# A graph layer and a mixture-of-experts layer on one core: the sum of squares by four transposes and a DVE sum, five second-choice scatters in two steps, pads, waits and the stage change rearranged

## The chip, the cores and the metric

The kernel runs on one core of one Trainium2 chip. The metric is the device time of one execution in microseconds (us), here as the median of several runs. The profile is of one execution; its span runs from the first to the last instruction.

## What is computed

`x` is 128 graphs of 64 nodes with 128 features (8192 tokens), `adj` a 64x64 matrix for each graph. Everything is float32.

```python
# first layer, on the layernorm of x
agg = epsilon * xn + adj @ xn
h = silu(rmsnorm(agg @ W1 + b1) * rms_weight)        # 512 wide
x = x + h @ W2 + b2
# second layer, on the layernorm of the new x: 8 experts, top 2
logits = xf @ Wg + bg
top_w, top_i = top_k(logits, 2);  top_w = softmax(top_w)
out = sum over e of w_dense[:, e] * (gelu(xf @ W1[e] + b1[e]) @ W2[e] + b2[e])   # exact gelu
x = x + out
```

## The kernel before

Each engine has its own instruction list, written by hand and joined by semaphores; no scheduler moves anything. There are two stages.

**Stage one** works on G = 16 groups of 512 tokens, one step `s` for each, in a software pipeline. TensorE (PE) aggregates group `s+3` (`aggregate`, L566), multiplies group `s+2` with the quadratic form of W1 (`quadratic`, L574), sums the products over the 128 features (`sum_squares`, L582), runs the first matmul of group `s+1` (`first_layer`, L600) and the residual and second matmul of group `s` (L607, L614). The mean square of the rmsnorm comes from that quadratic form: DVE multiplies `agg` with it (`product`, L851), `sum_squares` sums `prod` over the partitions, DVE adds epsilon (`mean_square`, L855), and GpSimd raises it to the power -1/2 (`pow_step(s)`, L435), together with the variances of both layernorms: 12 numbers per partition for s = 1 to 11, 8 for s = 12 to 14, 4 at s = 15. `spread` (L592) turns the result into a row for all partitions, by four transposes into bank 6 (QR_BANK), and `scale_agg` (L861) applies it before `first_layer` may start. `sum_squares` writes into bank 7 (SM_BANK), which it shares with `prefix` (L623 to L628), so it waits until DVE has read the last prefix (`prefix_used`).

DVE also takes the new `x` (`take_x2`, L867), normalizes, picks the two experts of each token, and turns counts from `prefix(s-1)` into row numbers (`rank_rows`, L921, and `place_rows`). In DVE's list, a loop step begins with `take_x2(s-1)`, its statistics and `mean_square(s+1)`, and ends with `rank_rows(s-1)`, which needs the `prefix(s-1)` that PE issues at the end of step `s`.

GpSimd scatters the rows of each token to two tables in device memory, by indirect DMA (`dispatch`, L446): four per group for the first choice, four for the second. First choices go out two steps later, and beside them three second choices per step from step 3 on (42 of 64 by the end). ScalarE (ACT) does silu, tanh and copies.

**Stage two** runs tiles of 128 table rows through the expert of the tile: 71 tiles of first choices, then 71 of second choices. The sync queue (SP) loads tile `i` into one of RING = 16 slots (`load_slots`, L358) once the output of tile `i-16` has been written (`added`). DVE normalizes the rows four tiles ahead (`norm_slots(i+4)`, L1052), copies the expert's W1 (`copy_block(i+3)`, L1046) and forms the output (`finish(i)`, L1121 and L1128 or L1131). PE turns the tile (`turn`, L686), then does layer 1 (L693) and layer 2 (L708). GpSimd writes the output by indirect DMA: a plain store for first choices (L458), an accumulating one for second choices (L461). Between the stores it issues the four first choices of the last group (before tiles 11 to 14) and the 22 second choices that are left: two in five tiles. Before tile 71 it waits for all 71 stores, since accumulation comes on top of them.

Unused rows at the end of each of the 16 regions (8 experts, two choices) are overwritten with `pad_rows` by SP (`pad`, L351). These 16 pads stand behind the loads of tiles 24 to 39, one behind each; the load of tile 40 waits until all have landed.

At the start ("prologue") the blocks of `adj` for groups 0 to 3 are placed by GpSimd (`place_adj`, L273), those of later groups by DVE.

The rhythm of SP in stage two before:

```python
for i in range(RING, EARLY):            # 16 to 39
    load_slots(i)
    if i >= EARLY - KE:                 # 24
        pad(i - (EARLY - KE))
sp.wait_ge(padded, 16 * (KE + TOP_K))
```

## Time and profile before

| | |
|---|---|
| median of 3 runs | 490.04 us (488.69 to 491.08) |
| profiled execution | 489.22 us |
| its span | 487.3 us |
| PE busy | 468.2 us, 96% of the span |
| DVE busy | 352.8 us, 72% |
| GpSimd (POOL) busy | 357.5 us, 73% |
| ACT busy | 263.5 us, 54% |
| granted TensorE clock, mean | 0.993 |

The profiled time is the span and 1.9 us around it. Busy shares are means over the two stages, which have different limits; a matmul in float32 shows as two records. "issue" is idle time for which the profile names no releaser.

### The profile page before, as it was taken

To read this page: it belongs to the slowest core of one execution; us is meant where nothing else is said; L and a number is where in the kernel's file an instruction comes from. 1 tells how busy PE (TensorE), PEld (TensorE's weight loads), DVE (VectorE), ACT (ScalarE), POOL (GpSimd) and SP (SyncE) were. 2 spreads that over 40 slices of the span, in tenths; PEclk is the share of its full clock that TensorE was granted. 3 is DMA by queue.
4 is the path that set the end of the run, shared out by engine and by line. 5 is a ranking of instruction groups with operands and counts; after the bars stand their busy time and mean duration, and the time that the engine had idled before them with its cause. 6 is when DMAs were issued, how large, how long until landed. Compare 5 with 4: busy or idle time off the path is not lost. (4 is left out here: it accounts for less than half of the span.)

```text
span 487.3 us, 14189 instructions
## 1 busy us (share of the span) xinstructions
PE 468.2 (96%) x3715; PEld 423.1 (87%) x3715; DVE 352.8 (72%) x1476; ACT 263.5 (54%) x829; POOL 357.5 (73%) x318
## 2 busy tenths in 40 slices
PE   8999999999999999799999899999999999999990
PEld 5687888877888877799999799999999999999990
DVE  6788888887887675698866576766767676776751
ACT  2333333333333324477777577777777777777770
POOL 4622577787877777777777777777588888888884
PEclk9999999999999999999999999999999999999997
DMA  5995122222222212332343343333254555555430
GB/s 178 363 316 178 57 72 79 73 77 62 67 68 65 78 45 65 84 80 85 97 113 107 97 112 86 86 89 91 44 69 68 73 72 73 72 69 71 55 33 6
DMA packets 54436, 44.78 MB, mean 92 GB/s; under 512 B 9506, under 2 KB 46024, under 8 KB 54360
## 3 DMA queue, kind: packets, MB, share of 16 engines
q1 hardware_dynamic: 36480, 26.11, 20.3%
q0 software_dynamic: 16592, 17.13, 17.5%
q8 instruction: 35, 0.57, 0.5%
q10 hardware_dynamic: 1288, 0.62, 0.5%
q14 instruction: 41, 0.34, 0.3%
HBM read 25.49 MB, written 19.25 MB: 92 GB/s over the span
## 5 line engine op out<-in xcount | busy, mean ns | idle before, releaser
L797 ACT ACTIVATE gelu_t<-ps,block_w 128x128 f32<-128x128 f32 x568 | 162.0, 368 | 35.9 <-PE ps L693 35.4
L446 POOL DMA_INDIRECT dispatched_rows<-payload,row_idx x128 | 124.9, 976 | 37.4 <-issue 35.9
L693 PE MATMUL ps<-slot_t,block_w 128*128 128x128 f32 x1136 | 150.7, 275 | 0.9 <-ACT gelu_t L797 0.4
L708 PE MATMUL ps<-experts,gelu_t 128*128 x1136 | 150.4, 275 | 0.4 <-ACT gelu_t L797 0.4
L693 PEld LDWEIGHTS ps<-slot_t,block_w 128*128 128x128 f32 x1136 | 138.1, 192 | 1.9 <-issue 0.8
L708 PEld LDWEIGHTS ps<-experts,gelu_t 128*128 128x128 f32 x1136 | 138.2, 192 | 0.8 <-issue 0.8
L461 POOL DMA_INDIRECT out_y<-y_out,slot_rows x71 | 112.6, 1585 | 24.6 <-issue 24.6
L458 POOL DMA_INDIRECT out_y<-y_out,slot_rows x71 | 72.0, 1015 | 23.7 <-issue 18.8
L1121 DVE TENSOR_TENSOR y_bias<-ps,block_w 128x128 f32<-128x128 f32 x142 | 41.4, 291 | 65.3 <-PE ps L708 63.5
L1046 DVE COPY block_w<-experts 128x644 f32 x142 | 73.0, 514 | 1.3 <-issue 1.3
L614 PE MATMUL ps<-w2e,hidden 128*128 128x136 f32 x512 | 69.6, 279 | 0.0
L1052 DVE TENSOR_SCALAR slot_n<-slot_rows 128x128 f32<-128x128 f32 x142 | 58.6, 414 | 8.1 <-DMA slot_rows<-dispatched_rows 7.9
L614 PEld LDWEIGHTS ps<-w2e,hidden 128*128 128x128 f32 x512 | 63.9, 190 | 0.0
L757 ACT ACTIVATE hidden<-ps,vec_cols 128x512 f32<-128x512 f32 x64 | 44.0, 687 | 32.8 <-PE ps L600 32.7
L791 ACT COPY slot_t<-ps 128x128 f32<-128x128 f32 x142 | 37.6, 265 | 40.7 <-PE ps L686 40.2
L600 PE MATMUL ps<-agg_r,w1b 128*128 128x512 f32 x128 | 59.1, 603 | 0.0
L435 POOL TENSOR_TENSOR powers<-powers_in,neg_half 128x12 f32<-128x12 f32 (+2 forms) x17 | 33.8, 1985 | 23.3 <-DVE powers_in L855 22.1
L600 PEld LDWEIGHTS ps<-agg_r,w1b 128*128 128x128 f32 x128 | 23.0, 190 | 22.6 <-issue 22.5
L686 PE MATMUL ps<-ident,slot_n 128*128 128x128 f32 x142 | 38.9, 275 | 3.3 <-DVE slot_n L1052 3.3
L770 ACT ACTIVATE agg<-ps,ones 128x512 f32<-128x512 f32 x16 | 11.0, 687 | 52.4 <-PE ps L566 52.4
L1131 DVE TENSOR_SCALAR y_out<-y_bias,slot_rows 128x128 f32<-128x128 f32 x71 | 31.1, 438 | 2.5
L607 PEld LDWEIGHTS ps<-ident_wg,xs_t 128*128 128x128 f32 x128 | 20.5, 190 | 13.9 <-issue 13.9
(146 smaller groups left out, 416.7 us busy)
## 6 DMA issues: line engine op xcount, KB each, us to landing
slot_rows<-dispatched_rows SPq DMA_DIRECT2D x142, 66.5 KB
xs<-in_x SPq DMA_DIRECT2D x16, 256.0 KB, 5.9
xs_t<-in_x_t SPq DMA_DIRECT2D x16, 256.0 KB, 3.1
experts<-in_f_w SPq DMA_DIRECT2D x16, 256.0 KB, 5.2
out_y<-y_out,slot_rows POOLq DMA_INDIRECT x142, 3.2
adj_in<-in_adj_t SPq DMA_DIRECT2D x16, 128.0 KB, 4.3
dispatched_rows<-payload,row_idx POOLq DMA_INDIRECT x128, 2.5
dispatched_rows<-pad_rows SPq DMA_DIRECT2D x18, 66.5 KB
```

The lines of the kernel that those rows point to most:

```text
L446: pool.indirect_dma_start(rows[k], bass.IndirectOffsetOnAxis(row_idx[:, g, j * TOP_K + k:j * TOP_K + k + 1], 0), payload[:, g * JT + j, 0: ...
L458: pool.indirect_dma_start(out, token, y_out[:, r, :], None, bounds_check=T - 1, oob_is_err=False).then_inc(added[r], 16)
L461: pool.indirect_dma_start(out, token, y_out[:, r, :], None, bounds_check=T - 1, oob_is_err=False, compute_op=ALU.add).then_inc(added[r], 16)
L600: pe.matmul(bank(n % H_BANKS, 0, GROUP), w1b[:, c * P:(c + 1) * P], agg_r[:, s % 2, :], start=True, stop=True).then_inc(h_done, 1)
L614: mm = pe.matmul(x2_part(j), hidden[:, c, j * P:(j + 1) * P], w2e[:, c, :], start=False, stop=(c == C - 1))
L693: mm = pe.matmul(bank((2 * i + c // 2) % FH_BANKS, c % 2 * SLOTS, SLOTS), block_w[:, i % BLOCKS, c * P:(c + 1) * P], slot_t[:, i % 2, :], ...
L708: mm = pe.matmul(bank(Y_BANK + i % 2, 0, P), gelu_t[:, i % 2, c, :], experts[:, bass.ds(at + (OW2 + c * P), P)], start=(c == 0), stop=(c = ...
L757: act.activation(hidden[:, c, :], ps[:, (C * s + c) % H_BANKS, :], ACT.Silu, scale=vec_cols[:, GRW + c:GRW + c + 1]).then_inc(hidden_ready, 1)
L797: act.activation(gelu_t[:, i % 2, c, :], ps[:, (2 * i + c // 2) % FH_BANKS, c % 2 * SLOTS:(c % 2 + 1) * SLOTS], ACT.Gelu, bias=block_w[:, ...
L1046: dve.tensor_copy(block_w[:, i % BLOCKS, :], experts[:, bass.ds(at, OW2)]).then_inc(block_ready, 1)
L1052: dve.tensor_scalar(slot_n[:, i % (AHEAD + 1), :], row[:, X2:WID], row[:, MEAN:MEAN + 1], row[:, RSTD:RSTD + 1], ALU.subtract, ALU.mult).t ...
L1121: dve.tensor_tensor(y_bias[:, i % 2, :], ps[:, Y_BANK + i % 2, 0:P], block_w[:, i % BLOCKS, OB2:OB2 + P], ALU.add).then_inc(y_chain, 1)
```

## The change

- `sum_squares` no longer multiplies with a column of ones. It transposes the four 128x128 pieces of `prod` into bank 6, and DVE sums each over its 128 features (a `tensor_reduce` of 128x512 from PSUM to 128x4) before it adds epsilon. Its wait for `prefix_used` goes; `prefix` takes it instead. `sum_squares(1)` moves behind the first half of `first_layer(0)`, since bank 6 is in use until then.
- DVE places `adj` of groups 0 to 3 as well, each while GpSimd computes the power of that group; statistics of group 3 move behind the norm of group 2.
- GpSimd issues five second choices in two steps (3 and 2 in turn) in stage one, 35 in all; 29 are left for stage two, three in five tiles.
- The wait for all stores is split: before each of tiles 63 to 69 GpSimd waits for two earlier stores (before tile 69: those of 67 and 68), and before tile 71 for those of 69 and 70.
- SP writes the 8 pads of the first choices behind every second load from 24 on, and the other 8 behind every third load from 42 on.
- At the stage change: ACT loads the table for gelu after its tanh in step 15; DVE copies the expert block of tile 0 in step 14 and normalizes tiles 0 and 1 ahead of the gate of step 15, tiles 2 and 3 and two more blocks behind it.
- ACT loads `b1_row` ahead of `w1g`.

```diff
@@ -178,12 +179,17 @@
         H_BANKS, X2_BANK, AGG_BANK, QR_BANK, SM_BANK = 3, 3, 5, 6, 7
-        MS, PR, TO = 0, 64, 192
+        PR, TO = 64, 192
         LAST_GATE, LAST_RANKS, LAST_FIRSTS = 9, 9, 11
         SECONDS_FROM = 3
-        SECONDS_LEFT = 3 * (G + 1 - SECONDS_FROM)
+        def second_of(s):
+            return (5 * (s - SECONDS_FROM) + 1) // 2
+        SECONDS_LEFT = second_of(G + 1)
         TURN_BANK, Y_BANK, FH_BANKS = 5, X2_BANK, 3
...
@@ -260,21 +265,6 @@
             return 0 <= g < G
-        def wait_adj(engine, g):
-            if g < PLACED:
-                engine.wait_ge(adj_placed, g + 1)
-            else:
-                engine.wait_ge(adj_ready, g - PLACED + 1)
-        def half_of_adj(engine, g, h):
-            half = slice(h * NODES, (h + 1) * NODES)
-            return engine.tensor_tensor(
-                adj_blocks[half, g % 4, :, half], adj_in[half, g % ADJ_RING, :, :],
-                eps_ident[half, half].rearrange("p (a n) -> p a n", a=1).to_broadcast([NODES, JT, NODES]),
-                ALU.add)
         def after(engine, semaphore, value):
...
@@ -372,15 +362,19 @@
                 load_slots(i)
-                if i == EARLY - KE:
+                if i == EARLY - 2 * E:
                     sp.wait_ge(ends_ready, 1)
-                if i >= EARLY - KE:
-                    pad(i - (EARLY - KE))
+                if i >= EARLY - 2 * E and i % 2 == 0:
+                    pad((i - (EARLY - 2 * E)) // 2)
             sp.wait_ge(tables_ready, 1)
-            sp.wait_ge(padded, 16 * (KE + TOP_K))
+            sp.wait_ge(padded, 16 * (E + TOP_K))
             sp.wait_ge(late_dispatched, 16 * JT * (G - EARLY_GROUPS))
...
                 load_slots(i)
+                if i % 3 == 0 and (i - EARLY) // 3 < E:
+                    pad(E + (i - EARLY) // 3)
+            sp.wait_ge(padded, 16 * (KE + TOP_K))
             sp.wait_ge(second_dispatched, 16 * JT * G)
...
@@ -411,14 +405,6 @@
                                    ALU.pow).then_inc(rstd1_ready, 1)
-            def place_adj(g):
-                pool.wait_ge(adj_loaded[g], 16)
-                half_of_adj(pool, g, 0).then_inc(adj_half, 1)
-                pool.wait_ge(adj_half, g + 1)
-                half_of_adj(pool, g, 1).then_inc(adj_placed, 1)
-                pool.wait_ge(adj_placed, g + 1)
             def pow_rms0():
...
@@ -461,12 +447,10 @@
                                             oob_is_err=False, compute_op=ALU.add).then_inc(added[r], 16)
+            def wait_written(i):
+                pool.wait_ge(added[i % RING], 16 * (i // RING + 1))
             pow_ln1(0)
-            pool.wait_ge(adj_clear, 1)
-            pool.wait_ge(eps_ready, 1)
-            pool.wait_ge(rstd1_ready, 1)
-            place_adj(0)
-            place_adj(1)
             pow_ln1(1)
...
@@ -474,14 +458,8 @@
             pow_rms0()
-            pool.wait_ge(pool_consts, 5)
-            pool.wait_ge(rrms_ready, 1)
-            place_adj(2)
             pow_step(0)
             pow_ln1(2)
-            pool.wait_ge(powers_ready, 1)
-            pool.wait_ge(rstd1_ready, 3)
-            place_adj(3)
             pow_ln1(3)
...
@@ -491,27 +469,32 @@
                 if s >= SECONDS_FROM:
-                    second(3 * (s - SECONDS_FROM))
+                    second(second_of(s))
                 if s == G:
...
                 if s >= SECONDS_FROM:
-                    second(3 * (s - SECONDS_FROM) + 1)
-                    second(3 * (s - SECONDS_FROM) + 2)
+                    second(second_of(s) + 1)
+                    if second_of(s) + 2 < second_of(s + 1):
+                        second(second_of(s) + 2)
             for i in range(NT):
...
                     dispatch(G - 1, i - LAST_FIRSTS, 0)
-                n = SECONDS_LEFT + (i - 1) // 5 * 2 + (i % 5 == 3)
-                if i % 5 in (1, 3) and n < G * JT:
+                n = SECONDS_LEFT + i // 5 * 3 + i % 5 // 2
+                if i % 5 in (0, 2, 4) and n < G * JT:
                     second(n)
+                if TILES - 8 <= i < TILES - 1:
+                    wait_written(2 * i - TILES)
+                    wait_written(2 * i - TILES + 1)
                 if i == TILES:
-                    for q in range(RING):
-                        pool.wait_ge(added[q], 16 * len(range(q, TILES, RING)))
+                    wait_written(TILES - 2)
+                    wait_written(TILES - 1)
                 write_tile(i)
...
@@ -560,7 +543,7 @@
                 pe.wait_ge(xn_ready, g + 1)
-                wait_adj(pe, g)
+                pe.wait_ge(adj_ready, g + 1)
                 after(pe, agg_copied, g)
...
@@ -575,12 +558,12 @@
                 pe.wait_ge(prod_ready, g + 1)
-                after(pe, ms_ready, g)
-                after(pe, prefix_used, g - 2)
+                if g == 1:
+                    pe.wait_ge(agg_r_ready, 1)
                 for j in range(JT):
-                    mm = pe.matmul(bank(SM_BANK, MS + j, 1), prod[:, j * P:(j + 1) * P], ones[:, 0:1],
-                                   start=True, stop=True)
+                    mm = pe.transpose(bank(QR_BANK, j * P, P), prod[:, j * P:(j + 1) * P], ident[:])
                 mm.then_inc(ms_done, 1)
...
@@ -617,7 +600,7 @@
                 pe.wait_ge(chosen_ready, g + 1)
-                pe.wait_ge(ms_ready, min(g + 3, G))
+                after(pe, prefix_used, g)
                 ch = chosen[:, g % 2, :]
...
@@ -649,12 +632,12 @@
             spread(0)
-            sum_squares(1)
             for s in range(G):
...
                     first_layer(0, (0, 1))
+                    sum_squares(1)
                     setup_gate()
...
@@ -725,8 +708,8 @@
         def _(act):
+            act.dma_start(b1_row, g_b1).then_inc(b1_loaded, 16)
             act.dma_start(w1g, g_w1).then_inc(w1_loaded, 16)
-            act.dma_start(b1_row, g_b1).then_inc(b1_loaded, 16)
             act.dma_start(eps_col[:], epsilon.to_broadcast([P, 1])).then_inc(eps_loaded, 16)
...
@@ -782,6 +765,9 @@
                     tanh(s - 1)
+                if s == G - 1:
+                    act.activation(table_warm[:], ones[:, 0:1], ACT.Gelu)
                 if live(s + 3):
...
@@ -839,10 +826,15 @@
                 for h in range(P // NODES):
-                    m = half_of_adj(dve, g, h)
+                    half = slice(h * NODES, (h + 1) * NODES)
+                    m = dve.tensor_tensor(
+                        adj_blocks[half, g % 4, :, half], adj_in[half, g % ADJ_RING, :, :],
+                        eps_ident[half, half].rearrange("p (a n) -> p a n", a=1).to_broadcast([NODES, JT, NODES]),
+                        ALU.add)
                 m.then_inc(adj_ready, 1)
...
@@ -852,7 +844,9 @@
                 dve.wait_ge(ms_done, g + 1)
-                dve.tensor_scalar(mean_sq_of(g), ps[:, SM_BANK, MS:MS + JT], RMS_EPS, RMS_EPS,
+                squares.link(dve.tensor_reduce(sum_sq[:], ps[:, QR_BANK, :].rearrange("p (j d) -> p j d", j=JT),
+                                               AX.X, ALU.add))
+                dve.tensor_scalar(mean_sq_of(g), sum_sq[:], RMS_EPS, RMS_EPS,
                                   ALU.add, ALU.max).then_inc(ms_ready, 1)
...
@@ -1052,11 +1046,15 @@
                                   ALU.subtract, ALU.mult).then_inc(slots_normed, 1)
-            dve.memset(adj_blocks[:], 0.0).then_inc(adj_clear, 1)
+            clear = Chain(dve, clear_chain)
+            clear.link(dve.memset(adj_blocks[:], 0.0))
             stats1_of(0)
+            dve.wait_ge(eps_ready, 1)
+            place_adj(0)
             norm1(0)
...
             stats1_of(1)
+            place_adj(1)
             norm1(1)
...
@@ -1066,14 +1064,14 @@
             stats1_of(2)
-            stats1_of(3)
+            place_adj(2)
             norm1(2)
             setup_w2()
+            stats1_of(3)
+            place_adj(3)
             norm1(3)
...
             stats1_of(4)
-            dve.wait_ge(adj_clear, 1)
-            dve.wait_ge(eps_ready, 1)
             place_adj(4)
...
@@ -1092,6 +1090,10 @@
                     early_table_1()
+                if s == G - 1:
+                    norm_slots(0)
+                    norm_slots(1)
                 if live(s - 1):
...
@@ -1104,13 +1106,16 @@
                     product(s + 2)
+                if s == G - 2:
+                    first_at = expert_of(dve, 0)
+                    second_at = expert_of(dve, 1)
+                    third_at = expert_of(dve, 2)
+                    copy_block(0, first_at)
                 if s == G - 1:
-                    copy_block(0, expert_of(dve, 0))
-                    copy_block(1, expert_of(dve, 1))
-                    copy_block(2, expert_of(dve, 2))
-                    for i in range(AHEAD):
-                        norm_slots(i)
+                    copy_block(1, second_at)
+                    norm_slots(2)
+                    norm_slots(3)
+                    copy_block(2, third_at)
                 if live(s - 1):
...
                     place_rows(s - 1)
```

PE's list at the start of step 0 (`prod` is the product for the sum of squares, `rrms` the reciprocal root mean square), before:

```order
L550 MATMUL ps<-ident,w2e 128x128 x4
L592 MATMUL ps<-ident,rrms 128x128 x4
L582 MATMUL ps<-ones,prod 128x1 x4
L600 MATMUL ps<-agg_r,w1b 128x512 x2
L557 MATMUL ps<-ident_wg,block_w 128x8 x4
L558 MATMUL ps<-ident_wg,b_rows 128x8
L600 MATMUL ps<-agg_r,w1b 128x512 x2
```

and with the change:

```order
L533 MATMUL ps<-ident,w2e 128x128 x4
L575 MATMUL ps<-ident,rrms 128x128 x4
L583 MATMUL ps<-agg_r,w1b 128x512 x2
L566 MATMUL ps<-ident,prod 128x128 x4
L540 MATMUL ps<-ident_wg,block_w 128x8 x4
L541 MATMUL ps<-ident_wg,b_rows 128x8
L583 MATMUL ps<-agg_r,w1b 128x512 x2
```

The sum of squares of group 1 has moved from ahead of the first `first_layer` pair to behind it, and its four matmuls are 128 columns wide.

DVE's list from the scaling of group 0 on, before:

```order
L861 TENSOR_TENSOR agg_r<-agg,ps 128x512
L855 TENSOR_SCALAR powers_in<-ps 128x4
L820 BN_STATS stats<-xs 128x6 x4
L823 BN_AGGR mv<-stats 128x2 x4
L826 TENSOR_SCALAR var<-mv 128x4
L820 BN_STATS stats<-xs 128x6 x4
L823 BN_AGGR mv<-stats 128x2 x4
L826 TENSOR_SCALAR var<-mv 128x4
L837 TENSOR_SCALAR xn<-xs,mv,rstd 128x128 x4
L965 COPY w2e<-ps 128x4x8
L966 COPY b_all<-ps 128x8
L837 TENSOR_SCALAR xn<-xs,mv,rstd 128x128 x4
```

and with the change:

```order
L855 TENSOR_TENSOR agg_r<-agg,ps 128x512
L847 TENSOR_REDUCE sum_sq<-ps 128x4
L849 TENSOR_SCALAR powers_in<-sum_sq 128x4
L807 BN_STATS stats<-xs 128x6 x4
L810 BN_AGGR mv<-stats 128x2 x4
L813 TENSOR_SCALAR var<-mv 128x4
L834 TENSOR_TENSOR adj_blocks<-adj_in,eps_ident 64x4x64 x2
L824 TENSOR_SCALAR xn<-xs,mv,rstd 128x128 x4
L959 COPY w2e<-ps 128x4x8
L960 COPY b_all<-ps 128x8
L807 BN_STATS stats<-xs 128x6 x4
L810 BN_AGGR mv<-stats 128x2 x4
```

The sum and the epsilon of group 1 are the second and third row. Behind them the statistics of group 3 have moved from ahead of the norm of group 2 to behind it, and a placing of `adj` stands before each norm.

GpSimd's list at the first tiles of stage two (`dispatched_rows` are scatters, `out_y` the stores of tiles), before:

```order
L435 TENSOR_TENSOR powers<-powers_in,neg_half 128x4
L446 DMA dispatched_rows<-payload,row_idx 66688x133 x4
L458 DMA out_y<-y_out,slot_rows 8192x128
L446 DMA dispatched_rows<-payload,row_idx 66688x133
L458 DMA out_y<-y_out,slot_rows 8192x128 x2
L446 DMA dispatched_rows<-payload,row_idx 66688x133
L458 DMA out_y<-y_out,slot_rows 8192x128 x3
L446 DMA dispatched_rows<-payload,row_idx 66688x133
L458 DMA out_y<-y_out,slot_rows 8192x128 x2
```

and with the change:

```order
L421 TENSOR_TENSOR powers<-powers_in,neg_half 128x4
L432 DMA dispatched_rows<-payload,row_idx 66688x133 x4
L444 DMA out_y<-y_out,slot_rows 8192x128 x2
L432 DMA dispatched_rows<-payload,row_idx 66688x133
L444 DMA out_y<-y_out,slot_rows 8192x128 x2
L432 DMA dispatched_rows<-payload,row_idx 66688x133
L444 DMA out_y<-y_out,slot_rows 8192x128
L432 DMA dispatched_rows<-payload,row_idx 66688x133
L444 DMA out_y<-y_out,slot_rows 8192x128 x2
L432 DMA dispatched_rows<-payload,row_idx 66688x133
```

Three scatters now fall on five tiles, where there were two.

## Rows read from the trace of the kernel before

**Rows 1.** Busy time by stretch: us, then busy us (count) of each engine, clock, DMA share, GB/s.
```profile
54.00:168.00 114.00, 114.00 (x779) 89.92 (x777) 92.27 (x520) 37.36 (x70) 87.66 (x78) 1.00 0.25 71
...
199.00:206.00 7.00, 4.33 (x32) 3.73 (x32) 4.58 (x18) 4.18 (x13) 5.17 (x7) 1.00 0.34 82
```

**Rows 2.** Timeline, one step: start, us, engine, line, operation (count) [idle before, releaser].
```profile
111.20 0.19 PE L623 MATMUL ps<-chosen,before 128*128 128x64 bf16 x1
...
112.38 0.95 PE L582 MATMUL ps<-ones,prod 128*128 128x1 f32 x8
...
114.92 0.15 DVE L855 TENSOR_SCALAR powers_in<-ps 128x4 f32<-128x4 f32 x1
...
115.17 2.33 POOL L435 TENSOR_TENSOR powers<-powers_in,neg_half 128x12 f32<-128x12 f32 x1 [0.34 <-DVE powers_in L855]
...
118.10 0.60 PE L592 MATMUL ps<-ident,powers 128*128 128x128 f32 x4
...
122.64 0.19 PE L623 MATMUL ps<-chosen,before 128*128 128x64 bf16 x1
```

**Rows 3.** Groups of instructions by form: count, busy us, mean ns, idle before.
```profile
L851 DVE TENSOR_TENSOR prod<-agg,ps 128x512 f32<-128x512 f32 x16 | 11.0, 688 | 10.6 <-PE ps L574 10.0 <-DVE next_row L958 0.5
...
L273 DVE TENSOR_TENSOR adj_blocks<-adj_in,eps_ident 64x256 f32<-64x256 f32 x24 | 10.0, 417 | 0.2
...
L435 POOL TENSOR_TENSOR powers<-powers_in,neg_half 128x8 f32<-128x8 f32 x3 | 5.0, 1678 | 2.2 <-DVE powers_in L855 2.2
...
L930 DVE TENSOR_REDUCE row_f<-row_cand 128x8 f32<-128x64 f32 x16 | 3.5, 220 | 0.5
```

**Rows 4.** Timeline of the prologue and the first step.
```profile
7.03 2.60 DVE L837 TENSOR_SCALAR xn<-xs,mv,rstd 128x128 f32<-128x128 f32 x4 [1.16 <-POOL rstd L411]
...
19.43 1.98 PE L600 MATMUL ps<-agg_r,w1b 128*128 128x512 f32 x4
...
24.46 1.16 PE L566 MATMUL ps<-adj_blocks,xn 128*128 128x128 f32 x8 [0.22 <-DVE xn L837]
...
32.46 0.78 DVE L867 TENSOR_TENSOR payload<-ps,b_all 128x272 f32<-128x272 f32 x2
...
34.91 2.30 POOL L435 TENSOR_TENSOR powers<-powers_in,neg_half 128x12 f32<-128x12 f32 x1 [4.04 <-DVE powers_in L855]
...
38.00 0.60 PE L592 MATMUL ps<-ident,powers 128*128 128x128 f32 x4
```

**Rows 5.** Timeline of TensorE, DVE and the sync queue in the expert stage.
```profile
266.50 0.27 PE L686 MATMUL ps<-ident,slot_n 128*128 128x128 f32 x1
...
270.05 0.34 SPq L358 DMA_DIRECT2D slot_rows<-dispatched_rows  x1
...
272.89 0.41 DVE L1052 TENSOR_SCALAR slot_n<-slot_rows 128x128 f32<-128x128 f32 x1 [1.26 <-DMA slot_rows<-dispatched_rows]
...
281.48 0.27 PE L686 MATMUL ps<-ident,slot_n 128*128 128x128 f32 x1
...
344.04 0.27 PE L686 MATMUL ps<-ident,slot_n 128*128 128x128 f32 x1
```

**Rows 6.** Timeline around the stores of tiles 0, 71 and 141.
```profile
206.11 0.35 DVE L1128 SCALAR_TENSOR_TENSOR y_out<-y_bias,slot_rows 128x128 f32<-128x128 f32 x1
...
209.31 1.08 POOL L435 TENSOR_TENSOR powers<-powers_in,neg_half 128x4 f32<-128x4 f32 x1 [1.16 <-DVE powers_in L884]
...
215.85 1.00 POOL L458 DMA_INDIRECT out_y<-y_out,slot_rows  x1 [0.30 <-issue]
...
348.02 1.57 POOL L461 DMA_INDIRECT out_y<-y_out,slot_rows  x1 [3.22 <-issue]
...
480.38 1.55 POOL L461 DMA_INDIRECT out_y<-y_out,slot_rows  x1 [0.30 <-issue]
```

**Rows 7.** Waits of GpSimd: us in total, times, longest.
```profile
POOL out_y L458 <- DVE y_out L1128: 4.9, 10, 0.9
```

**Rows 8.** DMA issues of the page: count, median us to landing.
```profile
out_y<-y_out,slot_rows POOLq DMA_INDIRECT x142, 3.2
```

More of the change, by code:

```diff
@@ L66, in moe_gnn @@
     GRW, GB2, FB1 = 0, C, C + 1
-    XT_RING, ADJ_RING, PLACED = 4, 8, 4
+    XT_RING, ADJ_RING = 4, 8
     AHEAD = 4
@@ L129, in moe_gnn @@
         mean_sq0 = sb("mean_sq0", [P, JT])
+        sum_sq = sb("sum_sq", [P, JT])
         rrms0 = sb("rrms0", [P, JT])
@@ L202, in moe_gnn @@
         eps_ready = sem("eps_ready")
+        clear_chain = sem("clear_chain")
         ln1_chain = sem("ln1_chain")
@@ L207, in moe_gnn @@
         xn_ready = sem("xn_ready")
-        adj_clear = sem("adj_clear")
-        adj_half = sem("adj_half")
-        adj_placed = sem("adj_placed")
         adj_ready = sem("adj_ready")
@@ L216, in moe_gnn @@
         ms_done = sem("ms_done")
+        ms_chain = sem("ms_chain")
         ms_ready = sem("ms_ready")
@@ L340, in _ @@
                 if g + XT_RING < G:
-                    wait_adj(sp, g + XT_RING - ADJ_RING)
+                    sp.wait_ge(adj_ready, g + XT_RING - ADJ_RING + 1)
                     load_adj(g + XT_RING)
@@ L815, in _ @@
             setup = Chain(dve, setup_dve)
+            squares = Chain(dve, ms_chain)
             def stats1_of(g):
```

## The prediction

> **What bounds the kernel now.** I read the busy time by stretch first, to see which engine is full where. In the middle of stage one PE is busy for all of 114 us and DVE for 81% of them; at the stage change PE works 4.33 of 7.00 us [rows 1]. So stage one is PE's, and about 2.7 us lie in the stage change. Then the timeline of one step: from `prefix` at 111.20 to the next at 122.64 is 11.44 us [rows 2], and this repeats ten times. The reader should follow a second loop through the same rows: after `prefix`, DVE ranks, takes x2 and ends with the epsilon at 114.92; GpSimd starts the power at 115.17 and needs 2.33 us, to 117.50; PE reaches `spread` at 118.10, 0.6 us later, and from there it takes 4.54 us to the next `prefix`. This loop is 6.30 + 0.05 (for the signal, my estimate) + 4.54 = 10.9 us long, only 0.55 us shorter than PE's own.
>
> In stage two a tile takes (344.04 - 281.48) / 33 = 1.896 us of PE [rows 5]. Between the turns of tiles 35 and 41, at 266.50 and 281.48, six tiles take 14.98 us in place of 11.37: 3.6 us lost to pads, with DVE waiting for slots (1.26 us before 272.89). GpSimd is the quiet limit. Its first store starts at 215.85, 9.7 us after the output of tile 0 was formed (206.11); its first accumulation at 348.02; its last at 480.38 [rows 6]. The latter are 70 intervals of 1.891 us, the tile's own period, and the execution ends with them. How long one operation of its list is: 97 lie between 215.85 and 348.02 (71 stores, 22 second choices, 4 first). Off the 132.2 us go the 2.9 us by which the idle time of 3.22 before the first accumulation exceeds the usual 0.30, and 1.9 us of waits for outputs (4.9 us less ten times 0.30 [rows 7]). That leaves 127.4 / 97 = 1.313 us.
>
> **Stage one, steps.** Removed: four matmuls by ones, 0.95 us. Added: four transposes, priced by those of `spread`, 0.60 us [rows 2]. PE saves 0.35 us a step. Added on DVE: the sum of 128x512. Its nearest rows are a sum of 128x64 at 0.220 us and a 128x512 operation reading PSUM at 0.688 us [rows 3]. I take 0.69 us plus 0.03 for the link; the bounds are 0.58 and 0.87. It stands between the statistics and the power, so it lies in the second loop: 10.89 + 0.72 = 11.61 us. That is above PE's 11.44 - 0.35 = 11.09. The cover of 0.6 us is gone and PE waits in front of `spread`: +0.17 us in each of the ten steps 2 to 11, +1.7 us. In steps 12 to 14 the power is 0.65 us shorter (1678 ns [rows 3] against 2.33 us), the loop 10.96, and PE saves its 0.35 us: -1.05 us in all.
>
> The Trainium skill (VectorE: DVE Perf Modes, Rules for kernel authors) speaks against this edit: expect `tensor_reduce` at one element per cycle, and restructure rather than put it on a hot path. No row here shows a sum of this size.
>
> **Prologue.** The placings leave GpSimd. That ends a contention: four norms took 2.60 us at 7.03 [rows 4] beside them. PE's setup matmuls lie over most of this; I take 0.2 us. But `sum_squares(1)` now follows the first pair of `first_layer(0)`, which starts at 19.43 and takes 1.98 us [rows 4]. DVE is free at 19.4 and used to go on at once. Now it waits to about 21.5 (less those 0.2) and adds 0.72 us of sum: it stands 2.9 us later, at 22.3. Behind it stand the statistics, the norm of group 2 and PE's `aggregate(2)`, which starts at 24.46 and would come near 26.1. The added placings (two instructions of 0.42 us each [rows 3] per group) hide under the powers, and the norms lose their contention, so the 13 us of DVE's list to `take_x2(0)` at 32.46 stay 13 us. `take_x2(0)` comes at 35.2. The power that followed it ended at 37.21; now 2.7 + 0.72 us later, at 40.6, and `spread` at 40.7 in place of 38.00: +2.7 us. Bounds: +1.2 (PE's list alone) and +3.2.
>
> Stage one and prologue: +2.7 + 1.7 - 1.05 = **+3.35 us** at the last `prefix`.
>
> **Stage change and pads.** Both gains are real for PE, up to 2.7 and 3.6 us. They don't reach the end, because GpSimd's list doesn't get shorter. Against the end of stage one:
> - The power of group 15 no longer waits for DVE: -1.2 us [rows 6].
> - Seven second choices come over from stage one. One takes the place of a third one in step 16, so six more operations lie between the first store and tile 71: 6 x 1.313 = +7.9 us.
> - No wait for an output any more, since GpSimd is always late: -1.9 us [rows 7].
> - A wait for a store just issued costs its landing. At tile 71 this was 3.22 + 0.98 = 4.20 us from store to store. Now it stands there and again before tile 69 (for store 68), at 3.9 us each for 1.31: 5.2 - 2.9 = +2.3 us. The landing has 3.2 us as its median [rows 8].
>
> First accumulation: **+7.1 us**. Before it, PE is held back too. In five tiles GpSimd needs 8 x 1.313 = 10.5 us where PE needs 9.5, plus four first choices. Store 0 would lag 11.2 us, store 15 about 19 us and store 47 more than 24 us behind its output. Slot `i` is loaded after store `i-16`, from store to issue to landing to norm about 5.9 us (3.2 [rows 8] and 2.8, from 270.05 to 272.89 [rows 5]); norms run 11 tiles ahead of that store's output, with some 2.3 us to spare on DVE. A lag over about 17.5 us therefore stops PE: some 7 us by tile 63, which take back the gains at the stage change and the pads. From tile 48 on GpSimd catches up 0.58 us a tile.
>
> Accumulations: 70 intervals at 1.891 us as before. The last ones, with DVE done, come at 1.85 us, so a queue that is late could win 0 to 3 us; I take -1.3.
>
> **Sum**: 489.2 + 3.35 + 7.1 - 1.3 = 498.4 us. The profiled execution lies 0.8 us below the median of the runs, so I say **499 us**. A measurement of this kernel can tell about 0.5% from no change: 487.6 to 492.5.
>
> **The rivals.**
> - *Same, 492 us.* The sum is cheaper or overlaps more, the second loop stays under 11.09 us, and the prologue costs 1.2 us: 1.2 - 13 x 0.35 = -3.35, 6.7 us less than forecast. For it: the margin is 0.5 us in a loop of 11.6. Against: every link of the loop is in the rows. 13%.
> - *Faster, 485 us.* One mechanism: GpSimd's list isn't the bound. Its place is tiles 0 to 47; it decides at 1.896 / 1.6 = 1.185 us per operation. If part of the 1.313 us is a wait on something that eases (the traffic of the pads, say), GpSimd keeps pace, -2.7 and -3.6 reach the end, and accumulations start when due, -2.4: 490.0 + 3.35 - 8.7. For it: 1.313 us is a mean, and what it holds can't be seen singly in it. Against: it stands over 97 operations, and would have to fall by a tenth. 17%.
> - *Slower still, 504 us.* A placing of `adj` on DVE doesn't run beside the power but waits for it: four times 0.83 us, and no drift at the end: 499.2 + 3.3 + 1.3. Against: 24 placings at 417 ns [rows 3], those of the loop beside powers. 8%. By the Trainium skill (SBUF — State Buffer, SBUF: two separate sides) DVE with two SBUF inputs and a GpSimd operation that reads SBUF exclude each other, which would make this the likely case; the trace's even 417 ns does not bear it out.
> - *The edits don't do what they say.* Pads and stage change may well be cured and show nothing. That is in the forecast.
>
> **The numbers.** Forecast 62%. Slower by over 0.5% takes the forecast and the third rival: 70%. Same 13%, faster 17%. The range runs from 488, which leaves most of the faster case out, to 505: sum at 0.87 us and prologue at its bound (+2.3 us), no drift (+1.3) and 1.35 us per GpSimd operation (+3.7), not all at once.
>
> **What would show it.** Steps 2 to 11 of 11.6 us, with PE idle before `spread`, waiting for the power. `aggregate(2)` near 26 us. No gap around the pads, but DVE waiting for slots between tiles 30 and 63. GpSimd without a wait from the stage change to tile 69, first accumulation 10 us later than before, last one 7 to 9 us behind its output. Wrong if steps take 11.1 us, or if stores catch up with their outputs before tile 48.

## The result: 503.0 us, slower, and the profile after

The changed kernel took 503.02 us (median of 4 runs, 502.42 to 503.80), the one before 490.56 beside it (4 runs, 488.69 to 491.12): a ratio of 1.026, 95% interval 1.023 to 1.029. The forecast was 499 us, with 488 to 505 as its range. The profiled execution has a span of 502.0 us, 14.7 more than before. Five of the runs below fell on two chips on which the kernel before itself took 612 and 605 us, with steps of up to 19.6 us from the third on, so their profiles are compared only ahead of 58 us; all other runs had the kernel before at 489.2 to 490.7 us beside them.

The windows of the changed kernel: the prologue, the middle of stage one, and the stage change. The second and third answer to [rows 1].

```profile
core 0: us, PE busy (x) PEld busy (x) DVE busy (x) ACT busy (x) POOL busy (x), PEclk, DMA share, GB/s
19.00:34.00 15.00, 12.90 (x68) 10.12 (x69) 10.54 (x48) 3.44 (x5) 4.02 (x4) 0.89 1.06 350
54.00:168.00 114.00, 110.03 (x728) 84.13 (x727) 99.18 (x530) 36.98 (x70) 82.60 (x73) 1.00 0.23 69
203.00:210.00 7.00, 5.88 (x56) 5.46 (x55) 5.27 (x23) 5.21 (x18) 5.39 (x6) 1.00 0.30 82
```

PE is no longer full in stage one (110 of 114 us), and it works 5.9 of 7 us at the stage change where it worked 4.3. One step, as in [rows 2]:

```profile
115.91 0.19 PE L606 MATMUL ps<-chosen,before 128*128 128x64 bf16 x1
...
119.52 0.17 DVE L878 TENSOR_SCALAR powers_in<-payload 128x4 f32<-128x4 f32 x1
119.60 0.68 DVE L847 TENSOR_REDUCE sum_sq<-ps 128x4 f32<-128x512 f32 x1
120.32 0.17 DVE L849 TENSOR_SCALAR powers_in<-sum_sq 128x4 f32<-128x4 f32 x1
120.57 2.34 POOL L421 TENSOR_TENSOR powers<-powers_in,neg_half 128x12 f32<-128x12 f32 x1 [0.48 <-DVE powers_in L849]
...
122.97 0.65 PE L575 MATMUL ps<-ident,powers 128*128 128x128 f32 x4 [0.44 <-POOL powers L421]
...
127.56 0.19 PE L606 MATMUL ps<-chosen,before 128*128 128x64 bf16 x1
```

The step is 11.65 us long, and PE stands 0.44 us in front of `spread`, released by the power. The new sum, 0.68 us, lies between the statistics and the power. In the prologue, against [rows 4]:

```profile
19.21 1.98 PE L583 MATMUL ps<-agg_r,w1b 128*128 128x512 f32 x4 [0.78 <-DVE agg_r L855]
...
21.67 0.69 DVE L847 TENSOR_REDUCE sum_sq<-ps 128x4 f32<-128x512 f32 x1 [2.51 <-PE ps L566]
...
26.35 1.82 PE L549 MATMUL ps<-adj_blocks,xn 128*128 128x128 f32 x8 [1.88 <-DVE xn L824]
...
28.88 1.68 PE L597 MATMUL ps<-w2e,hidden 128*128 128x136 f32 x8
...
41.52 0.65 PE L575 MATMUL ps<-ident,powers 128*128 128x128 f32 x4 [0.27 <-POOL powers L421]
```

DVE waits 2.51 us for `sum_squares(1)`, then PE waits 1.88 us for DVE; eight matmuls of `aggregate(2)` take 1.82 us and eight of the second layer 1.68 (1.05 to 1.14, and 1.09, in later steps). From 26.66 to 30.07 us the granted clock is 0.50, the lower level (1.2 GHz). Last, GpSimd's list, against [rows 6]: the first store, the last ones before tile 71, the first accumulation (line L447) and the last.

```profile
220.42 1.00 POOL L444 DMA_INDIRECT out_y<-y_out,slot_rows  x1 [0.30 <-issue]
...
354.13 0.98 POOL L444 DMA_INDIRECT out_y<-y_out,slot_rows  x1 [0.81 <-DVE y_out L1136]
357.41 1.06 POOL L444 DMA_INDIRECT out_y<-y_out,slot_rows  x1 [2.30 <-DVE y_out L1136]
358.77 1.27 POOL L444 DMA_INDIRECT out_y<-y_out,slot_rows  x1 [0.30 <-issue]
361.99 1.80 POOL L447 DMA_INDIRECT out_y<-y_out,slot_rows  x1 [1.95 <-DVE y_out L1136]
...
494.64 1.55 POOL L447 DMA_INDIRECT out_y<-y_out,slot_rows  x1 [0.30 <-issue]
```

DVE's named outputs had long been formed (that of tile 69 at 349.49): the gaps of 2.30 and 1.95 us are landings of the stores just issued. In the waits of the changed kernel (total, times, longest), DVE waits for slots 25 times (7 times, 7.9 us, before):

```profile
DVE slot_n L1046 <- DMA slot_rows<-dispatched_rows: 26.8, 25, 3.0
PE ps L575 <- POOL powers L421: 5.4, 12, 0.7
```

Where the 14.7 us went, read along these rows: last `prefix` +4.28 (198.66 to 202.94), from there to the first store +0.29, first store to first accumulation +9.40 (132.17 to 141.57), from there to the end +0.7. The last `prefix` is here and below the last one of stage one, that of group 14; the one of group 15 stands among the first tiles of stage two.

### The profile page after: what moved, and what is told of

Its sections match the earlier page's. It is cut to its first block, busy times and chain, and to the rows that moved or that the text cites. A ratio compares the mean times of both kernels' runs of the same rounds, so it can differ in the third digit from the quotient of the medians.

```text
span 502.0 us, 14057 instructions
## 1 busy us (share of the span) xinstructions
PE 468.9 (93%) x3651; PEld 419.7 (84%) x3651; DVE 365.3 (73%) x1500; ACT 264.4 (53%) x830; POOL 355.7 (71%) x310
## 2 busy tenths in 40 slices
DMA packets 54435, 44.76 MB, mean 89 GB/s; under 512 B 9506, under 2 KB 46024, under 8 KB 54360
## 4 chain that ended last, share of the span: by engine, by line
POOL 37%; PE 27%; issue 23%; DVE 6%; DMA 3%; ACT 1%; POOLq 1%; DVEq 0%; SPq 0%
POOL out_y L447 14%; POOL dispatched_rows L432 11%; PE ps L597 6%; PE ps L676 6%; PE ps L691 6%; POOL powers L421 6%; POOL out_y L444 5%; PE ps L575 2%; DMA out_y<-y_out,slot_rows 2%; PE ps L557 1%; DMA slot_rows<-dispatched_rows 1%; PE ps L590 1%; PE ps L583 1%; PE ps L549 1%; PE ps L669 1%
## 5 line engine op out<-in xcount | busy, mean ns | idle before, releaser
L432 POOL DMA_INDIRECT dispatched_rows<-payload,row_idx x128 | 126.7, 990 | 37.4 <-issue 32.5
L447 POOL DMA_INDIRECT out_y<-y_out,slot_rows x71 | 112.9, 1590 | 23.3 <-issue 21.3
L444 POOL DMA_INDIRECT out_y<-y_out,slot_rows x71 | 73.7, 1038 | 24.1 <-issue 19.8
L1046 DVE TENSOR_SCALAR slot_n<-slot_rows 128x128 f32<-128x128 f32 x142 | 56.9, 402 | 27.7 <-DMA slot_rows<-dispatched_rows 26.8
L583 PE MATMUL ps<-agg_r,w1b 128*128 128x512 f32 x128 | 58.0, 595 | 0.8 <-DVE agg_r L855 0.8
L740 ACT ACTIVATE hidden<-ps,vec_cols 128x512 f32<-128x512 f32 x64 | 44.0, 688 | 26.2 <-PE ps L583 26.1
L746 ACT COPY payload<-powers 128x4 f32<-128x4 f32 x16 | 3.2, 198 | 57.5 <-DVE gap L901 57.5
```

What stands on the lines that cost most here:

```text
L432: pool.indirect_dma_start(rows[k], bass.IndirectOffsetOnAxis(row_idx[:, g, j * TOP_K + k:j * TOP_K + k + 1], 0), payload[:, g * JT + j, 0: ...
L444: pool.indirect_dma_start(out, token, y_out[:, r, :], None, bounds_check=T - 1, oob_is_err=False).then_inc(added[r], 16)
L447: pool.indirect_dma_start(out, token, y_out[:, r, :], None, bounds_check=T - 1, oob_is_err=False, compute_op=ALU.add).then_inc(added[r], 16)
L583: pe.matmul(bank(n % H_BANKS, 0, GROUP), w1b[:, c * P:(c + 1) * P], agg_r[:, s % 2, :], start=True, stop=True).then_inc(h_done, 1)
L1046: dve.tensor_scalar(slot_n[:, i % (AHEAD + 1), :], row[:, X2:WID], row[:, MEAN:MEAN + 1], row[:, RSTD:RSTD + 1], ALU.subtract, ALU.mult).t ...
```

## The experiments

**Run a_sec, repeated as a_sec_again and a_sec_third: the second choices of the kernel before.**

```diff
-            return (5 * (s - SECONDS_FROM) + 1) // 2
+            return 3 * (s - SECONDS_FROM)
...
-                n = SECONDS_LEFT + i // 5 * 3 + i % 5 // 2
-                if i % 5 in (0, 2, 4) and n < G * JT:
+                n = SECONDS_LEFT + (i - 1) // 5 * 2 + (i % 5 == 3)
+                if i % 5 in (1, 3) and n < G * JT:
```

> The changed kernel with the second choices back at three per step and two in five tiles (42 in stage one, 22 left); all else as changed. Theory, GpSimd's list sets the end: six operations fewer between the first store and tile 71, 6 x 1.332 = -8.0 us, so the first accumulation near 354, the last near 486.6, and 495.0 us in all; the waits of DVE for slots in tiles 24 to 62 go. Rival one, the loss is stage one's and the prologue's (the last prefix is 4.3 us later) and GpSimd only looks late: 501 to 503 us. Rival two, the extra landing waits at tiles 63 to 71 are what costs: the time falls by less than 3 us, and the gaps of 3.3 us before tiles 69 and 71 stay the larger part of the lag.

> The same kernel as in the first run (the changed kernel with 42 and 22 second choices), since the kernel before took 612 us on the chip of the first runs, with steps of stage one of 16.9 us. Theory, GpSimd's list, on a chip where the kernel before takes 490: first accumulation near 354, last near 486.6, 495.0 us. Rival, stage one and prologue: 501 to 503 us.

> The kernel of the first run once more (the changed kernel with 42 and 22 second choices), for a chip where the kernel before takes 490 us. Theory, GpSimd's list: six operations less, first accumulation near 354, last near 486.6, 495.0 us. Rival, stage one and prologue alone: 501 to 503 us.

The first two fell on the chips of 612 and 605 us (ratios 1.008 and 1.014) and settle nothing of this. The third: 496.73 us, ratio 1.012 (1.007 to 1.017), so 6.3 us below the changed kernel, with the last `prefix` as late as there (203.35). Its first accumulation comes at 355.90. PE lost 1.0 us in tiles 24 to 63 where the changed kernel lost 9.9. One landing was longer than any in the forecast, store 68 to store 69 in 5.08 us:

```profile
346.60 0.98 POOL L444 DMA_INDIRECT out_y<-y_out,slot_rows  x1 [0.98 <-issue]
351.68 0.98 POOL L444 DMA_INDIRECT out_y<-y_out,slot_rows  x1 [4.11 <-DVE y_out L1136]
```

Rival one falls, and so does rival two, by which less than 3 us were to be won. Most of the miss of 1.7 us against 495.0 is that landing.

**Runs b_sec and b_sec_again: the kernel before with only the new counts** (the diff above the other way round).

> The kernel before with only the new counts of second choices (five in two steps, three in five tiles). Theory, GpSimd's list: six operations more, +7.9 us, less the 1.9 us of waits for outputs that go, so the first accumulation near 354 and 496.6 us in all; steps of stage one stay at 11.44 us. Rival one, GpSimd's list has room: 490 to 491 us. Rival two, fewer operations in stage one shorten its steps: 488 us.

> The kernel before with only the new counts of second choices (35 and 29), once more, for a chip where the kernel before takes 490 us. Theory, GpSimd's list: +7.9 us of operations less the 1.9 us of waits for outputs, 496.6 us, first accumulation near 354, lag of the stores over 17 us in tiles 15 to 45, and PE held back there. Rival one, GpSimd's list has room: 490 to 491 us. Rival two, shorter steps of stage one: 488 us.

On the chip of 612 us this edit cost nothing (0.997, interval 0.995 to 1.000): the outputs come so slowly there that GpSimd waits 56.8 us for them. The second run took 495.37 us, ratio 1.011 (1.007 to 1.015), +4.6 us, first accumulation at 354.04. Its steps stay at 11.44 us, so both rivals fall. Its stores lag up to 19.3 us, and PE loses 8.4 us in tiles 24 to 63 (the kernel before, with the same pads, 3.6).

**Run a_ones: the sum of squares by ones again, places unchanged.**

```diff
-                    mm = pe.transpose(bank(QR_BANK, j * P, P), prod[:, j * P:(j + 1) * P], ident[:])
+                    mm = pe.matmul(bank(SM_BANK, MS + j, 1), prod[:, j * P:(j + 1) * P], ones[:, 0:1],
+                                   start=True, stop=True)
...
-                squares.link(dve.tensor_reduce(sum_sq[:], ps[:, QR_BANK, :].rearrange("p (j d) -> p j d", j=JT),
-                                               AX.X, ALU.add))
-                dve.tensor_scalar(mean_sq_of(g), sum_sq[:], RMS_EPS, RMS_EPS,
+                dve.tensor_scalar(mean_sq_of(g), ps[:, SM_BANK, MS:MS + JT], RMS_EPS, RMS_EPS,
```

> The changed kernel with the sum of squares by four matmuls by ones again, in the same places of the program, without transposes and without the sum on DVE. Theory, the sum of 0.69 us lengthens the loop DVE, power, spread: steps 2 to 11 go back from 11.64 to 11.44 us (-2.0), steps 12 to 14 lose their 0.4 us each (+1.2), the prologue gains the 0.72 us of the sum; the last prefix 1.5 us earlier, the time 501.5 us. Rival one, the sum costs nothing on the path: 503 us and steps of 11.64 us stay. Rival two, more matmul columns in stage one keep up TensorE's granted clock: the time rises above 503.

**Run a_ones_pos: besides, `sum_squares(1)` back behind `spread(0)`.**

> As the run with ones again, and sum_squares(1) put back behind spread(0), ahead of first_layer(0). Theory, its place makes DVE wait 2.5 us in the prologue, and PE comes back from that wait at a lower granted clock: aggregate(2) back near 24.5, the first spread of the steps near 38.2 instead of 41.5, 2.7 us off the run with ones alone: 498.8 us. Rival, the later start of the steps is due to the placings that moved to DVE and into its list: then aggregate(2) stays near 26 and the time at that of the run with ones.

Both ran on the chip of 612 us (0.999 and 0.994 against before), so the times that they forecast can't be judged, and only what comes ahead of 57 us is read. The profiled executions start up to 2 us apart, so I count from `first_layer(0)` to the first `spread` of the steps: before 38.00 - 19.43 = 18.57 us; changed 22.31; ones again 20.45; ones and the old place 18.09. The sum costs 1.86 us of the prologue, its place 2.36, and the other edits there, the placings on DVE among them, win 0.48. The first full step of the run with ones, from 44.76 to 56.20, is 11.44 us long, that of the changed kernel 11.60. `aggregate(2)` in that run:

```profile
26.47 1.16 PE L549 MATMUL ps<-adj_blocks,xn 128*128 128x128 f32 x8 [1.04 <-DVE xn L825]
```

PE's wait is 1.04 us in place of 1.88, the granted clock of 19 to 34 us stays at 1.00 (the changed kernel: 0.89), and the eight matmuls take 1.16 us. The chip is not the reason: a_sec, on the same one, has a wait of 1.89 us and 0.89. So of the 1.86 us only 0.39 come ahead of `aggregate(2)` (7.14 us after `first_layer(0)` in the changed kernel, 6.75 here), and 1.65 are the slower matmuls between it and the first `spread` (4.04 us for 2.39); 0.18 come back behind it. The clock was forecast for the place of `sum_squares(1)`; the sum alone brought it back. With the old place too, `aggregate(2)` comes 4.66 us after `first_layer(0)` (5.03 in the kernel before), so the rival, by which the placings on DVE hold it up, falls.

**Run a_best: these edits together** (ones, old place, 42 and 22 second choices).

> The changed kernel with ones again, sum_squares(1) ahead of first_layer(0), and 42 and 22 second choices: of the change there stay the placings on DVE, the stage change, the pads and the split wait for the stores. On a chip where the kernel before takes 490 us. Theory: the last prefix 5.6 us earlier than in the changed kernel (-4.8 by the first spread, -2.0 by ten steps, +1.2 by the last three), six operations less for GpSimd (-8.0): first accumulation near 348.4, the time 489.4, so no better than before, since two landing waits take what the stage change gives on GpSimd. Rival, PE is the bound once the lag of the stores is gone: the 2.0 us of the stage change and the 3.6 of the pads reach the end too, 484 to 486 us. On a chip with the steps of 16.9 us: below 608 us, the best of all there.

489.45 us beside 489.19, ratio 1.001 (0.999 to 1.003). All steps at 11.44 us, last `prefix` at 198.04, first accumulation at 348.88. Against the changed kernel the last `prefix` comes 4.9 us earlier, for 5.6. The rival falls: outputs come 6 us earlier than in the kernel before (71 at 338.63 against 344.57), and nothing of it reaches the end, since the stores are 7 to 17 us behind:

```profile
348.88 1.63 POOL L447 DMA_INDIRECT out_y<-y_out,slot_rows  x1 [3.75 <-DVE y_out L1135]
```

**Run b_late: the kernel before with only the stage change and the pads.**

> The kernel before with only the stage change and the pads of the change (waits for the stores together before tile 71, second choices 42 and 22). Theory: PE gains 5.6 us, but GpSimd's list gets shorter by its waits alone (about 0.6 to 1.2 us of the power of group 15, 1.9 us for outputs): 487.5 us, first accumulation near 345.5. Rival, GpSimd's list isn't the bound: all of the 5.6 us, 484.5 us.

489.80 us beside 490.48, ratio 0.998 (0.995 to 1.000). From the last `prefix` to output 71 it is 141.1 us in place of 145.9, a gain of 4.8 us for PE; from the last `prefix` to the first accumulation it is 148.8 in place of 149.4, a gain of 0.6. The gain is absorbed, more fully than I expected. One operation of GpSimd took 1.33 us here, for 1.31 in the kernel before; over 97 operations that is some 2 us, about what the forecast missed. The last `prefix` stands at 200.20 here; output 71 and the first accumulation:

```profile
341.31 0.29 DVE L1142 TENSOR_SCALAR y_out<-y_bias,slot_rows 128x128 f32<-128x128 f32 x1
...
349.00 1.63 POOL L464 DMA_INDIRECT out_y<-y_out,slot_rows  x1 [2.50 <-issue]
```

**Run a_wait: the changed kernel with all waits for stores together before tile 71.**

```diff
-                if TILES - 8 <= i < TILES - 1:
-                    wait_written(2 * i - TILES)
-                    wait_written(2 * i - TILES + 1)
                 if i == TILES:
-                    wait_written(TILES - 2)
-                    wait_written(TILES - 1)
+                    for q in range(TILES - RING, TILES):
+                        wait_written(q)
```

> The changed kernel with the waits for the stores all together before tile 71, as in the kernel before. Theory, of the two landings one goes: store 68 to 69 falls from 3.3 to 1.3 us, 70 to 71 rises by the 1 us that the sixteen waits take; 502.0 us, within 2 us of the changed kernel. Rival, the waits from tile 63 on are what makes GpSimd late: below 499 us.

502.17 us, ratio 1.024 (1.020 to 1.028), the changed kernel's own time within what can be measured. One landing went; the other took 4.89 us. The rival falls.

**Run a_best2: GpSimd's list made shorter.** To a_best two edits: the waits together, as above, and

```diff
-        SECONDS_FROM = 3
+        SECONDS_FROM = 2
```

> The kernel of the run a_best (ones again, sum_squares(1) ahead of first_layer(0), 42 and 22 second choices) with two more edits: the second choices start one step earlier, in step 2, so 45 lie in stage one and 19 are left; and the waits for the stores stand together before tile 71, as in the kernel before. Theory, GpSimd's list sets the end: three operations less after the first store, -3.9 us, and one landing wait less, -1.6 us: 489.4 - 5.5 = 483.9 us, first accumulation near 343.4. Rival one, PE is the bound by now: it moves by less than 2 us. Rival two, GpSimd is full in step 2 as well and holds up the power of step 3: the last prefix is later by the 1 to 3 us by which its list is too long, and the gain falls to half.

**482.80 us** beside 490.06, ratio 0.986 (0.984 to 0.989): the fastest kernel of this study, below both. The last `prefix` keeps its place (197.78), so GpSimd had room in step 2, and both rivals fall. The two edits were not run apart, and not all of the gain is theirs: the last landing took 3.05 us, against 4.72 in a_best. The third row is the first accumulation, 2.7 us ahead of its forecast:

```profile
336.34 0.98 POOL L444 DMA_INDIRECT out_y<-y_out,slot_rows  x1 [0.31 <-issue]
337.62 0.98 POOL L444 DMA_INDIRECT out_y<-y_out,slot_rows  x1 [0.30 <-issue]
340.68 1.57 POOL L447 DMA_INDIRECT out_y<-y_out,slot_rows  x1 [2.07 <-DVE y_out L1132]
```

**Run best2_old_stage: a_best2 with the old stage change and pads.**

> The kernel of the run a_best2 with the stage change and the pads as in the kernel before. Theory: their gains for PE (2.0 and 3.6 us) are real and were lost in the changed kernel only because GpSimd was late; in a_best2 it is 2.2 us behind at tile 69, so here output 70 comes at 336.06 + 5.6 = 341.7, the last store waits for it, and the time is 482.8 + 5.3 = 488.1 us. Rival, these edits give nothing wherever they stand: below 484.5 us.

487.79 us beside 490.48, ratio 0.997 (0.994 to 0.999), 5.0 us above a_best2. Output 70 comes at 341.80, for 341.7 forecast, and the last store waits for it as said:

```profile
341.80 0.35 DVE L1114 SCALAR_TENSOR_TENSOR y_out<-y_bias,slot_rows 128x128 f32<-128x128 f32 x1
342.94 0.98 POOL L440 DMA_INDIRECT out_y<-y_out,slot_rows  x1 [0.91 <-DVE y_out L1114]
```

The same two edits that gave 0.7 us on top of the kernel before (with an interval that reaches none) give 5.0 where GpSimd's list has room. Stage change and pads were not run apart.

The kernels in one table, times from their profiled executions (us). The lag of a store is its start less the start of the DVE operation that forms its output; "PE lost" is the time from the first matmul of tile 24 to that of tile 63, less 39 times 1.896 us:

| kernel | last prefix | first store | store lag at 15, 45 | PE lost, tiles 24 to 63 | output 71 | first accumulation | from there to the end |
|---|---|---|---|---|---|---|---|
| before | 198.66 | 215.85 | 13.3, 8.5 | 3.6 | 344.57 | 348.02 | 139.3 |
| changed | 202.94 | 220.42 | 19.9, 19.5 | 9.9 | 353.28 | 361.99 | 140.0 |
| a_sec_third | 203.35 | 220.96 | 15.7, 14.4 | 1.0 | 344.97 | 355.90 | 139.2 |
| b_sec_again | 199.23 | 216.55 | 17.1, 15.5 | 8.4 | 350.12 | 354.04 | 139.9 |
| a_best | 198.04 | 215.28 | 15.9, 14.1 | 0.3 | 338.63 | 348.88 | 139.3 |
| a_best2 | 197.78 | 214.71 | 16.0, 13.2 | 0.1 | 337.96 | 340.68 | 139.8 |
| best2_old_stage | 198.33 | 215.98 | 13.2, 8.8 | 2.6 | 343.69 | 345.99 | 140.1 |

The last column is the finding: whatever came before, the end of the span follows the first accumulation by 139.2 to 140.1 us.

## Why the prediction was right, step by step

The sign and the mechanism held, and the size within the range: 503.0 lies 4 us above the forecast, 12.5 us above the kernel before for 9. Between the profiled executions, for which the sum was worked out, it is 14.7 us for 9.2: 0.9 more at the last `prefix`, 1.5 from there to the first store, 1.1 from there to the first accumulation, 2.0 behind it. By its steps:

- **Steps of stage one.** Forecast 11.61 us for steps 2 to 11, measured 11.64; the sum 0.69 us as taken; PE waits for the power, 5.4 us in 12 times. Steps 12 and 13 gave back 0.44 us each and step 14 0.33, for 0.35 forecast.
- **The rival "same"** (second loop under 11.09 us) fell with these rows.
- **Prologue**: forecast +2.7, measured +3.5 at `spread` (41.52). `aggregate(2)` came at 26.35, as said (26.1). The step that failed is "the 13 us of DVE's list to `take_x2(0)` stay 13 us": they also wait for PE's matmuls, which ran at a lower clock after the wait of 1.88 us. From the sum (its end at 22.36) to `take_x2(0)` at 35.97 it is 13.6 us, and 0.57 us of it are the wait for the late `spread`:

```profile
31.03 0.69 DVE L855 TENSOR_TENSOR agg_r<-agg,ps 128x512 f32<-128x512 f32 x1 [0.57 <-PE ps L575]
...
35.97 0.78 DVE L861 TENSOR_TENSOR payload<-ps,b_all 128x272 f32<-128x272 f32 x2
```

  So +4.28 at the last `prefix`, for 3.35.
- **The power of group 15**, "no longer waits: -1.2 us": failed. The wait moved one power up the list,

```profile
199.49 1.07 POOL L421 TENSOR_TENSOR powers<-powers_in,neg_half 128x4 f32<-128x4 f32 x1 [1.14 <-DVE powers_in L878]
```

  and the way from the last `prefix` to the first store is 0.29 us longer, not shorter. The power of group 15 itself does start without a wait, at 213.85; by then the list was 0.9 us later against the last `prefix` than before, and the scatters between took longer.
- **GpSimd's list.** First accumulation +9.7 us beyond the last `prefix`, for +7.1. Besides the power, the mis-sized term is one operation: by the spacing of starts, with idle time above 0.30 us taken off, 1.31 us before and 1.33 in the changed kernel, 0.024 us more and so 2.5 us over 103 operations. The three kernels with the old stage change and pads lie at 1.30 to 1.31, the six with the new ones at 1.31 to 1.33; why is not shown. The six operations (7.9 us) are borne out by a_sec_third, and the two landings were shorter than forecast (3.28 and 3.22 us, for 3.9 each).
- **PE held back**: I said some 7 us by tile 63 once the lag passes 17.5 us. With the new pads, where the lag stays within 16.9 us PE loses 0.1 to 1.0 us (a_best2, a_best, b_late, a_sec_third), and at 21.5 it loses 9.9. b_sec_again, at 19.3, loses 8.4, of which the old pads cost 3.6 in the kernel before. So the bound lies where it was forecast, between 16.9 and 19.3, and the loss was larger. Part of it is the clock: after 1.94 us without a slot PE ran at the lower level from 265.59 to 269.00,

```profile
264.44 0.33 PE L669 MATMUL ps<-ident,slot_n 128*128 128x128 f32 x1 [1.94 <-DVE slot_n L1046]
...
266.10 1.91 PE L691 MATMUL ps<-experts,gelu_t 128*128 x8
```

  where the second row takes 1.06 us in other tiles.
- **Stage change and pads real but absorbed**: shown by b_late (0.7 us, of 4.8 that PE gained) and the pair a_best2 and best2_old_stage (5.0 us). PE alone gains 2.0 us at the stage change, for "up to 2.7".
- **The faster rival** (GpSimd keeps pace at 1.185 us per operation) fell: no kernel went below 1.30.
- **The third rival** (placings on DVE wait for the power) fell, though its 504 us lay nearest: two of them run in 0.85 us right beside a power that GpSimd has from 120.57 to 122.91,

```profile
121.43 0.85 DVE L834 TENSOR_TENSOR adj_blocks<-adj_in,eps_ident 64x256 f32<-64x256 f32 x2
```

  and the prologue's other edits won 0.48 us. The rule that I had weighed there, from the Trainium skill (SBUF — State Buffer, SBUF: two separate sides), is not borne out for this pair. A short power beside such a placing takes 1.11 us in the prologue of the changed kernel (24.04), for 1.01 alone.
- **Accumulations**: forecast -1.3 us of drift, measured none, see below. This term was wrong in kind.

## What to carry to other kernels

Look for the engine with the list that ends the program, even if it is busy 71% of the time, and price every edit by what it does to that list: here the span ends 140 us after the first accumulation. A gain on another engine is worth nothing until that list has room, and then it is worth all of it; so an edit that measures as no change should be tried again after the list was shortened. An operation moved from a full stage into a later one is only free if the later one has a slower need of that engine; here five tiles needed 10.5 us of GpSimd against 9.5 of PE, and the place with room was step 2.

## What the runs showed that I had not expected

**A late queue doesn't catch up.** In the changed kernel GpSimd is 9 us behind its outputs during all accumulations, and yet issues one per tile, every 1.895 us. Alone, with DVE done, it needs 1.85. Rows of a_best2 beside it (lag 2.7 us) and of the changed kernel at 422 us (lag 9):

```profile
405.09 1.59 POOL L447 DMA_INDIRECT out_y<-y_out,slot_rows  x1 [0.30 <-issue]
406.99 1.59 POOL L447 DMA_INDIRECT out_y<-y_out,slot_rows  x1 [0.30 <-issue]
```

```profile
421.12 1.55 POOL L447 DMA_INDIRECT out_y<-y_out,slot_rows  x1 [0.31 <-issue]
422.98 1.63 POOL L447 DMA_INDIRECT out_y<-y_out,slot_rows  x1 [0.30 <-issue]
424.91 1.55 POOL L447 DMA_INDIRECT out_y<-y_out,slot_rows  x1 [0.30 <-issue]
```

It never waits for an output (0.30 us of issue each time), but takes 1.59 us, or 1.55 and 1.63 by turns, and in the latter case DVE's own row beside the 1.63 is longer:

```profile
421.53 0.29 DVE L1136 TENSOR_SCALAR y_out<-y_bias,slot_rows 128x128 f32<-128x128 f32 x1
...
423.42 0.63 DVE L1136 TENSOR_SCALAR y_out<-y_bias,slot_rows 128x128 f32<-128x128 f32 x1
```

The two engines fall into step: their rows keep the same places to each other from tile to tile, and the accumulations keep the tile's period. Which holds which is not settled by the rows: at 477.95 us an accumulation of 1.55 us stands beside such a DVE row of 0.63. By the Trainium skill (SBUF — State Buffer, SBUF: two separate sides) a DVE operation in a two-port mode keeps GpSimd from writing the descriptors of its DMAs. That the accumulation takes 1.55 us once DVE is done fits it, but no run took the DVE operation away, so the cause stays argued. The period is shown: 1.889 to 1.895 us on average in nine kernels, at lags from 2.3 to 11 us.

**A lower clock behind a short wait.** After 1.88 us in which PE stood before `aggregate(2)`, the granted clock of 19 to 34 us reads 0.89, with the lower level from 26.66 to 30.07, and matmuls took up to 1.8 times as long; after 1.04 us in the run with ones it read 1.00. In the nine profiles of the table and of b_late and a_wait each fall to the lower level ahead of the last matmuls follows a single wait of PE of 1.53 to 2.05 us. But a wait of 1.73 us at the stage change of the kernel before and one of 2.14 us in best2_old_stage left the clock at 1.00, so the length of the wait alone doesn't decide it; that the wait is the cause is argued, not shown.

**Landings vary.** From a store just issued to the next behind a wait for it: 2.9 to 5.1 us over nine kernels, which by itself moves the end by 2 us.
